# A fused four-layer kernel: routing of the chunk in front spread over six steps of the last attention chunk, and half of the second expert matrices loaded earlier

## What is computed

```python
x = x + tanh(g_xattn[3]) * L3_xattn(layernorm(x), ctx, ...)
x = x + tanh(g_ffn[3]) * L3_ffn(layernorm(x), ...)

def L3_ffn(x, keys, w1, b1, w2, b2, rw, rb):
    logits = -sum((x[:, :, None, :] - keys) ** 2, -1) + einsum('bld,ed->ble', x, rw) + rb
    topv, topi = top_k(logits, 4)
    w = softmax(topv)
    hidden = gelu(einsum('bld,efd->blef', x, w1) + b1)
    exp_out = einsum('blef,edf->bled', hidden, w2) + b2
    return sum(w[..., None] * take_along_axis(exp_out, topi[..., None], axis=2), axis=2)
```

## Time and profile before

| | |
|---|---|
| median of three runs | 1583.37 us (1582.58 to 1584.12) |
| profiled execution: its own time, its span | 1582.47 us, 1580.70 us |
| TensorE busy, mean granted clock | 1380.3 us (87%), 0.964 |
| VectorE, ScalarE, GpSimd busy | 1102.3, 1015.8, 538.1 us |
| HBM read, written | 43.03 MB, 54.93 MB |
| `in_L_ffn_w` (expert matrices) to the arena | 8 loads of 1024 KB |
| the last chunk, first maxima to last | 1150.67 to 1203.43 us |
| first tile load of F3 | 1255.54 us |

### The profile page before, as it was taken

One profiled execution on the slowest core, in us unless ns is written; L12 is line 12 of the kernel. 1 busy time (PEld: TensorE's weight loads), 2 busy tenths in 40 slices (PEclk: granted clock), 3 DMA queues, 4 the chain that ended last, 5 costly groups with the idle time before them and its releaser, 6 DMA issues.

```text
span 1580.7 us, 34386 instructions
## 1 busy us (share of the span) xinstructions
PE 1380.3 (87%) x9974; PEld 1029.7 (65%) x9974; DVE 1102.3 (70%) x3531; ACT 1015.8 (64%) x2931; POOL 538.1 (34%) x640
## 2 busy tenths in 40 slices
PE   4788887988899988998999999999976299999994
PEld 3566665676744465443666666666666199999994
DVE  4788877687777667883666876776665466666665
ACT  2688887554555564225788777777764377777762
POOL 3363468222211411010003242242144445555550
PEclk9999999999999999999999999999987599999998
DMA  8100059500499910000000010010034122222227
GB/s 195 25 8 7 14 83 175 84 0 14 92 175 180 146 34 21 1 0 7 1 8 25 12 34 24 12 35 17 21 126 161 40 62 64 66 66 64 63 57 266
DMA packets 143412, 98.24 MB, mean 62 GB/s; under 512 B 20598, under 2 KB 132515, under 8 KB 142155
## 3 DMA queue, kind: packets, MB, share of 16 engines
q1 hardware_dynamic: 134602, 80.09, 25.6%
q0 software_dynamic: 8704, 16.87, 3.2%
HBM read 43.03 MB, written 54.93 MB: 62 GB/s over the span
## 4 chain that ended last, share of the span: by engine, by line
PE 61%; ACT 13%; DVE 11%; issue 10%; another core or an unknown queue 2%; DMA 1%; SPq 1%; POOL 0%; DVEq 0%; ACTq 0%; POOLq 0%
PE bank L1442 7%; PE bank L1450 7%; PE bank L1008 6%; PE bank L1294 4%; PE bank L1024 4%; ACT arena L1483 4%; PE bank L949 3%; ACT att L1620 3%; PE bank L1059 3%; PE bank L1012 2%; ACT att L1485 2%; PE bank L1044 2%; PE bank L1034 2%; PE bank L1370 2%
## 5 line engine op out<-in xcount | busy, mean ns | idle before, releaser
L1483 ACT ACTIVATE arena<-bank 128x512 f32<-128x512 f32 (+7 forms) x380 | 245.7, 675 | 151.4 <-PE bank L1357 54.0
L1900 ACT ACTIVATE att<-bank,arena 128x128 f32<-128x128 f32 x576 | 165.1, 372 | 71.2 <-PE bank L1442 69.9
L822 POOL DMA_INDIRECT expert_outputs<-arena x144 | 146.2, 1016 | 146.0 <-issue 105.1
L1620 ACT ACTIVATE att<-bank,arena 128x128 f32<-128x128 f32 x512 | 180.7, 395 | 17.8 <-DVE arena L2158 16.7
L776 POOL DMA_INDIRECT dispatched_rows<-arena x112 | 113.0, 1009 | 177.2 <-DVE arena L2047 116.2
L1450 PE MATMUL bank<-arena,att 128*128 128x128 f32 x1152 | 153.8, 277 | 2.7 <-ACT att L1900 1.5
L609 POOL TENSOR_TENSOR ve<-mv,eps 128x4 f32<-128x4 f32 x64 | 13.0, 202 | 417.6 <-DVE mv L1963 408.1
L1442 PE MATMUL bank<-xnT,arena 128*128 128x128 f32 x1152 | 154.1, 277 | 0.2 <-ACT xnT L1483 0.2
L1450 PEld LDWEIGHTS bank<-arena,att 128*128 128x128 f32 x1152 | 140.6, 192 | 5.2 <-ACT att L1900 5.2
L1442 PEld LDWEIGHTS bank<-xnT,arena 128*128 128x128 f32 x1152 | 141.6, 194 | 0.8 <-ACT xnT L1483 0.8
L2625 DVE COPY arena<-arena 128x512 f32 x144 | 61.9, 430 | 84.7 <-issue 84.2
(11 more groups left out here) (381 smaller groups left out, 3244.6 us busy)
## 6 DMA issues: line engine op xcount, KB each, us to landing
dispatched_rows<-padf SPq DMA_DIRECT2D x16, 2128.5 KB, 31.7
arena<-dispatched_rows SPq DMA_DIRECT2D x144, 64.5 KB
cxT<-in_ctx SPq DMA_DIRECT2D x32, 256.0 KB
arena<-in_L_ffn_w SPq DMA_DIRECT2D x8, 1024.0 KB
arena<-expert_outputs SPq DMA_DIRECT2D x8, 1024.0 KB, 14.2
expert_outputs<-arena POOLq DMA_INDIRECT x144
out_x<-x SPq DMA_DIRECT2D x8, 256.0 KB, 4.3
dispatched_rows<-arena POOLq DMA_INDIRECT x112
```

The costliest lines, as they stand in the source:

```text
L822: pl.indirect_dma_start(sent_out, bass.IndirectOffsetOnAxis(xtu3[:, s, P:P + 1], 0), yt3[:, s, :], None, bounds_check=TOP3 * TOKENS - 1, o ...
L1483: copy = lambda o, i: nc.scalar.activation(o, i, ACT.Copy)
L1620: last = nc.scalar.activation(ex3_of(w, side)[:, i, :], bank[side][:, i * P:i * P + P], ACT.Exp, bias=nm3[:, w % 2, h:h + 1], accum_out=su ...
L1900: last = nc.scalar.activation(h3[:, s % 2, k * P:k * P + P], bank[s % 2][:, k * P:k * P + P], ACT.Gelu, bias=b1c3[:, s % 4, k:k + 1])
```

## The change

Routing of chunk 6 beside chunk 7 gets one unit a step. On VectorE: 6 in step 2 behind the normalisations, 7 in step 3, 8 in 4, 9 in 5, 10 in 6, and 12 is cut in two: the places (13) in step 7, the weights (14) in the drain. On TensorE 8, 9 and 12 are in steps 3, 4 and 6, each behind the transposes of the probabilities; on ScalarE 8 in step 4 ahead of the copies, 9 in step 4 and 10 in step 6 behind them. The residual and statistics of chunk 7's first half move from the front of step 7's normalisations to behind them. In the drain, TensorE's and ScalarE's unit 8 of half 0 stands behind the transposes and copies of the probabilities.

The arena is laid out anew: `w2T3` lies so that its second eight experts cover `v3[0]`, the values of the even chunks, and the tiles `xt3` lie between `last3` and it. So SyncE loads these eight experts (two loads) when the last values of chunk 6 are multiplied, and the first eight (two loads) where all four were. Since `last3` now lies on the last chunk's keys, its first writers wait for all scores and no longer for chunk 6's values.

```diff
@@ -332,2 +332,3 @@
 qk3 = ar([P, 2, HEADS, W])
+values3_at = used[0]
 v3 = [ar([P, CB, HEADS, D3]) for _ in range(2)]
@@ -361,5 +362,11 @@
 fresh()
-w1T3, w2T3 = ar([P, E3, H3]), ar([P, E3, H3])
+w1T3 = ar([P, E3, H3])
 last3 = ar([P, SC, ROW3])
 lastu3 = arena[:, used[0] - SC * ROW3:used[0]].bitcast(U32).rearrange("p (q d) -> p q d", q=SC)
+at = used[0]
+xt3 = ar([P, SLOTS3, ROW3])
+xtu3 = arena[:, at:used[0]].bitcast(U32).rearrange("p (s d) -> p s d", s=SLOTS3)
+assert used[0] <= values3_at - E3 // 2 * H3
+used[0] = values3_at - E3 // 2 * H3
+w2T3 = ar([P, E3, H3])
 combined = arena[:, 0:NC * TOP3 * W].rearrange("p (c j k d) -> p c j k d", c=NC, k=TOP3, j=CB)
@@ -370,5 +377,2 @@
 tabf3, tab3 = ar([1, 2, NT]), ar([1, 2, NT], I32)
-at = used[0]
-xt3 = ar([P, SLOTS3, ROW3])
-xtu3 = arena[:, at:used[0]].bitcast(U32).rearrange("p (s d) -> p s d", s=SLOTS3)
 yt3 = ar([P, SLOTS3, P])
@@ -541,4 +545,7 @@
     sp.dma_start(w1T3[:, e:e + EL3, :], a["L3_ffn_w1"][:, e:e + EL3, :]).then_inc(s_w, 16)
+sp.wait_ge(sem("A3_pv"), (NC - 1) * PAIRS)
+for e in range(E3 // 2, E3, EL3):
+    sp.dma_start(w2T3[:, e:e + EL3, :], a["L3_ffn_w2"][:, e:e + EL3, :]).then_inc(s_w, 16)
 sp.wait_ge(sem("A3_scores"), NC * (2 * PAIRS))
-for e in range(0, E3, EL3):
+for e in range(0, E3 // 2, EL3):
     sp.dma_start(w2T3[:, e:e + EL3, :], a["L3_ffn_w2"][:, e:e + EL3, :]).then_inc(s_w, 16)
@@ -1080,8 +1087,10 @@
     routing(c - 1, {3: 8, 4: 9, 6: 12}[w])
-if live and not more and w in (3, 4, 5):
-    routing(c - 1, {3: 8, 4: 9, 5: 12}[w])
-if not live:
-    routing(c - 1, {0: 8, 1: 9, 2: 12}[w], 0)
+if not live and w:
+    routing(c - 1, {1: 9, 2: 12}[w], 0)
 if (live and w >= 1) or (not first and w < 1):
     probs_T(c, w - 1)
+if live and not more and w in (3, 4, 6):
+    routing(c - 1, {3: 8, 4: 9, 6: 12}[w])
+if not live and w == 0:
+    routing(c - 1, 8, 0)
 for s in mine[3:]:
@@ -1503,3 +1512,3 @@
     act.wait_ge(sem("F3_normalised"), c + 1)
-    act.wait_ge(sem("A3_pv"), (NC - 1) * PAIRS)
+    act.wait_ge(sem("A3_scores"), NC * (2 * PAIRS))
 copy(rows_of(half)[0][:, qs_of(js), 0:P].rearrange("p (j k) d -> p j k d", j=n),
@@ -1640,8 +1649,6 @@
     routing(c - 1, {3: 8, 5: 9, 6: 10}[w])
-if live and not more:
-    for u in {3: (8,), 5: (9, 10)}.get(w, ()):
-        routing(c - 1, u)
-if not live:
-    for u in {0: (8,), 1: (9,), 2: (10,)}[w]:
-        routing(c - 1, u, 0)
+if live and not more and w == 4:
+    routing(c - 1, 8)
+if not live and w:
+    routing(c - 1, {1: 9, 2: 10}[w], 0)
 for side in range(2):
@@ -1652,2 +1659,7 @@
             piece(c + 1, 1 - p, s)
+if live and not more:
+    for u in {4: (9,), 6: (10,)}.get(w, ()):
+        routing(c - 1, u)
+if not live and w == 0:
+    routing(c - 1, 8, 0)
 
@@ -2024,3 +2036,3 @@
 else:
-    dve.wait_ge(sem("A3_pv"), (NC - 1) * PAIRS)
+    dve.wait_ge(sem("A3_scores"), NC * (2 * PAIRS))
 step(v.tensor_copy(tags[:, qs, P:P + 1], goes3[:, qs].unsqueeze(2)))
@@ -2037,3 +2049,3 @@
     v.tensor_reduce(ohs3[:, of, :], oh3[:, qs, :].rearrange("p (j k) e -> p j e k", j=n), AX, ALU.add).then_inc(sem("F3_chosen"), 1)
-if u == 12:
+if u in (12, 13):
     dve.wait_ge(sem("F3_routing"), c * 3 + 3)
@@ -2047,3 +2059,3 @@
     v.tensor_copy(places[:, qs], to3[:, qs]).then_inc(sem("F3_rows_ready"), 1)
-
+if u in (12, 14):
     dve.wait_ge(sem("F3_exp"), c + 1)
@@ -2201,35 +2213,43 @@
 
-def body(c, p, more, first=False, live=True, ahead=True):
-    for w in range(PAIRS if live else DRAIN3):
-        if live:
-            maxima(c, w)
-        if w == 2 and not first and live:
+def last_body(c):
+    for w in range(PAIRS):
+        maxima(c, w)
+        if w == 2:
             residual(c - 1)
-        if live and not more:
-            for u in {2: (6,), 3: (7, 8), 5: (9, 10), 6: (12,)}.get(w, ()):
-                routing(c - 1, u)
-            if w == 7:
-                residual_half(c, 0)
-                routing(c, 6, 0)
-        if not live:
-            if w < 2:
-                values(c, w - 2)
-            for u in {0: (7, 8), 1: (9, 10)}.get(w, ()):
-                routing(c - 1, u, 0)
-            if w == 2:
-                residual_half(c - 1, 1)
-                routing(c, 6, 1)
-                routing(c - 1, 12, 0)
-            continue
-        if live and not first and more:
+        if w in (3, 4, 5, 6, 7):
+            routing(c - 1, {3: 7, 4: 8, 5: 9, 6: 10, 7: 13}[w])
+        values(c, w - 2)
+        for side in range(2):
+            normal(c, w, side)
+        if w == 2:
+            routing(c - 1, 6)
+    residual_half(c, 0)
+    routing(c, 6, 0)
+
+def drain(c):
+    routing(c - 2, 14)
+    values(c, -2)
+    routing(c - 1, 7, 0)
+    routing(c - 1, 8, 0)
+    values(c, -1)
+    routing(c - 1, 9, 0)
+    routing(c - 1, 10, 0)
+    residual_half(c - 1, 1)
+    routing(c, 6, 1)
+    routing(c - 1, 12, 0)
+
+def body(c, first=False, ahead=True):
+    for w in range(PAIRS):
+        maxima(c, w)
+        if w == 2 and not first:
+            residual(c - 1)
+        if not first:
             for u in {2: (6,), 3: (7,), 4: (8,), 5: (9,), 6: (10,), 7: (12,)}.get(w, ()):
                 routing(c - 1, u)
-        if (live and w >= 2) or (not first and w < 2):
+        if w >= 2 or not first:
             values(c, w - 2)
-        if live:
-            normal(c, w, 0)
-        if more and ahead and 3 <= w < 7:
+        normal(c, w, 0)
+        if ahead and 3 <= w < 7:
             front(c + 2, w - 3)
-        if live:
-            normal(c, w, 1)
+        normal(c, w, 1)
 
@@ -2241,8 +2261,8 @@
     front(1, k)
-body(0, 0, True, True)
+body(0, first=True)
 for c in range(1, NC - 2):
-    body(c, c % 2, True)
-body(NC - 2, 0, True, ahead=False)
-body(NC - 1, 1, False)
-body(NC, 0, False, live=False)
+    body(c)
+body(NC - 2, ahead=False)
+last_body(NC - 1)
+drain(NC)
 
```

## The result

The changed kernel takes 1587.78 us (median of 15 runs, 1581.08 to 1589.07), the kernel before, beside it, 1583.28 (15 runs, 1580.41 to 1585.2). The ratio is 1.0022, 95% interval 1.0014 to 1.0031 (it is worked out from all runs and is not the quotient of the two medians, 1.0028): 0.2% slower, where 0.2% faster was forecast, and above the range's upper end of 1584.5. The profiled execution took 1585.06 us with a span of 1582.9, against 1582.47 and 1580.70.

The account below looks back on a forecast made before the run. GpSimd's row scatters, which SyncE's first tile load waits for, were taken as the bound. A 3.9 us smaller gap between scatters, all else 0, gave 1582.47 - 3.9 = 1578.6 profiled, 1579.5 median; range 1575.8 to 1584.5.

Parts of the forecast that it names:

- w4 to w5: Last chunk, between VectorE's maxima of two steps: logits behind the transposes, same TensorE work, so length stays 6.15 us.
- the four steps: Last chunk's steps from w3 to w7: together 7.0 us shorter, maxima of w7 at 1196.4 instead of 1203.43.
- GpSimd starts where it did: Chunk 6's first scatter: places ready at 1200.4 as before; bounds 1.7 us later to 1.2 earlier.
- The hole: GpSimd's gap before its last sixteen scatters: from 6.51 us to 2.15, less 0.48, so 3.9 us gained.
- theory G: Posed in the experiments: remote stands of VectorE and ScalarE come from GpSimd's back-to-back scatters, where before takes some 1583 us.
- The 2.15 us: GpSimd's own need between two scatters, seen at 1206, 0.64 of it before two small operations; what the gap shrinks to.
- The drain: Behind the last chunk's steps: 22.24 us from w7's maxima to the last residual, 1 us allowed more, residual at 1219.6.
- my later bound: Drain with the places' 2.74 us in full: last half's variance at 1224.5, and 0.9 us of the gain gone.
- The rival of the load beside the values: Moved load stalls an engine in w1 to w3 by 5.2 us, giving 1584.7; chance 0.13.
- The split load is worth 0: Second matrices, two of four loads issued near 1160 instead of 1202.5: by themselves they bring 0.
- the steps keep their length: Rival: w7's maxima stay at 1203.43, places come 7.0 us later, 3.1 us slower, 1586.5; chance 0.1.
- The stand of 3.22 us: GpSimd's unexplained wait among the last sixteen scatters, kept in the sum; rival that it goes: 1576.3, chance 0.14.

Follow-up runs that it names:

- experiments 1 and 2: Changed kernel without TensorE's wait for ScalarE's routing-transpose copy: ratio 0.9990 to the kernel before; changed kernel, wait kept, that copy one step earlier: 1561.74 us, 0.9994.
- experiment 5: Changed kernel without TensorE's wait, chunk 6's routing moved about one step earlier: 1559.44 us, 0.9984 of the kernel before; on a slower chip 1579.55, 0.9975.
- experiment 1: Changed kernel without the last chunk's first projection waiting for ScalarE's copy of chunk 6's routing transposes: 1561.47 us, ratio 0.9990 to the kernel before.
- experiment 4: The kernel before, unchanged, traced on a chip of the faster kind: 1560.91 us, one run.
- experiment 1's repetition: Changed kernel without TensorE's wait 1560.70 us, 0.9994 of the kernel before; beside it the changed kernel as it is, 1567.45 us, 1.0038.

## Why the prediction was wrong

- **The step that failed** is "w4 to w5: logits behind the transposes instead of ahead, same work on TensorE in front of the same scores: 6.15". It measured 13.09. I had costed ScalarE's row copy in w4 (0.4 us in the bound), but put at nothing that its unit 8 came there too, behind eight exponentials, and had not asked who waits for it. TensorE's projection does, with the values behind it, which ScalarE and VectorE wait for. It cost 4.25 us of stand and, at the lower clock, 1.7 more for the projection and 0.9 for the values: 6.85 of the 6.94 us by which the step was mis-sized, and nearly all of the 7.0 that the four steps were to give. Shown by experiments 1 and 2, where the step with the wait took 11.55 us and without it, or with the copy in w3, 6.35 and 7.33; the version of experiment 5, on a chip of the slower kind, 6.79.
- **The other steps** of the sum were right within 0.7 us; without the wait, w4 to w5 too (6.35). "GpSimd starts where it did" came out in experiment 1, 0.65 us from the kernel before.
- **The hole** was to give 3.9 us and gave 1.8. In this size it exists only where the remote stands do; without them it is 1.55 us. I read its size off one execution and put VectorE's stand down to the load of the second matrices. By theory G it belongs to GpSimd's own scatters, though no run left out those of the drain: it stayed beside them when 96 others went, and beside them also in the changed kernel, at a later instruction of VectorE. The 2.15 us that GpSimd "itself needs" were misread as well: the 0.64 in it was a wait for the variance, as the row at 1192.55 in experiment 4 says.
- **The drain** was mis-sized: the 1 us that I allowed from the maxima of w7 to the last residual was 3.62 (25.86 us against 22.24), 1.42 of it the longer stand. Where there is no stand it was 1.57 (17.78 us in experiment 1's repetition against 16.21 in experiment 4). So even with the steps as forecast the last residual would have come later than 1219.6, by 2.6 us, and taken about the 0.9 us of my later bound.
- **The rival of the load beside the values** fell: its reading of the earlier trace rows was a coincidence. The same 5.2 us stand came in five chunks (918.95, 978.47, 1038.01, 1097.61, 1157.17), four times with no load of weights near. "What they wait for is rare" was wrong and could have been read from the trace of before.
- **The split load is worth 0**: right, 0.9993 with 1 inside the interval, measured on a chip without the stands.
- **The rival "the steps keep their length"** gave the right sign and nearly the time (1586.5), by luck, since its mechanism was wrong: the maxima of w7 came at 1202.56 because one step took back what four had given.
- **The stand of 3.22 us** was kept, rightly (3.14 in the changed kernel). It left this place when 24 scatters came in front and when 96 went.

## What to carry to other kernels

When a step is moved to a later place in one engine's queue, list every semaphore it raises and find each instruction that waits for one, also those far from the change: a credit for a shared bank can be waited for by work that has nothing to do with the moved step. Give such a wait up only where the two uses are in different banks. And before taking a stand as something to be won, look whether it comes back in every turn of the loop, and in a trace from another chip.

## What the hardware showed unexpectedly

- The same kernel takes 1582 to 1584 us on some chips and 1562 to 1563 on others (two of each kind in the experiments, each in one group of runs, so chip and moment are not told apart; which chip the first measurement had is not on record). Where it takes 1583, VectorE and ScalarE stand 2 to 7 us, labelled remote, while or just after GpSimd issues scatters back to back. In a chunk's stand the engines go on together, TensorE's products, which stop for a shorter time, at 1097.37 us, VectorE at 1097.61 and ScalarE at 1097.65. Beside 24 scatters in a row VectorE stood 4.5, 11.6 and 10.7 us. Without 96 of the scatters 14.4 us went. Where it takes 1562, the same scatters stall nobody. What differs, wasn't found. The Trainium skill (Trainium Architecture — The Big Picture, What this means for kernel authors) names an exclusive lock between VectorE and GpSimd on a shared port; that can't be all of it here, since ScalarE stands too (13.59 us) and the stands depend on the chip.
- GpSimd stands 3.1 to 3.4 us ahead of its 114th scatter in eleven traces, and with 24 scatters put in front the wait at the new 114th grew by about as much (6.54 us with some 3 of another wait in it). With 96 left out no such stand was seen, at the 114th or within the last sixteen. The cause is open.
- A stand of 4.25 us of TensorE cost more than itself: the 16 products behind it took 3.75 us at the lower clock (0.50 granted) and not 2.0 to 2.2.
